# A fused four-layer kernel: FP4 decoding and an output projection moved between the attention and MLP stages, and a changed division of SSM passes in one batch

## Chip, cores and metric

The kernel runs on one core of one Trainium2 chip. The metric is device microseconds for one execution of the whole program. Five engines work side by side: TensorE (PE; PEld is its weight load), VectorE (DVE), ScalarE (ACT), GpSimd (POOL) and SyncE (SP, which here only issues transfers).

## What is computed

`x` is 4 batches of 512 rows by 512 columns in fp32. Four layers are added to it one after another:

```
x = x + ssm(ctx, layernorm(x))            # state-space scan, 512 channels, 16 states
x = x + experts(layernorm(x))             # top-1 of 32 masked ternary matrices
x = x + attention(layernorm(x), ctx)      # 32 heads of 16, softmax, @ Wout + bout
x = x + mlp(layernorm(x))                 # FP4 weights
# mlp: gate_up = x @ w_gu.T   (512 -> 2 x 1408);  h = silu(gate) * up
#      y = h @ w_down.T;  y / sqrt(mean(y*y) + 1e-6)
# FP4: eight 4-bit codes in an int32 word; value = code's number * fp16 scale of its group of 128
```

## The kernel before

The program is a row of stages: SSM, experts, attention, MLP. A stage is one or more blocks. In a block each engine has an instruction stream of its own and waits on semaphores; at a block's end the engines meet at a barrier, before which SP clears the block's semaphores one by one. `X` stays in SBUF as 16 tiles of 128 rows, 4 to a batch.

**SSM.** 128 passes g: 4 batches (32 passes each, g = 96 to 127 are the last batch) by 2 halves of the channels by 16 states. A pass has two 128x512 tiles, w = 0 and 1. ACT makes `dA` for both (L327); POOL makes `dBu` for both in one 128x1024 product (`weigh_states`, L363); DVE runs two scans (L464), and multiplies tile 0 by C into `hC` (L419); tile 1 is multiplied by POOL (`project`, L370), except in a *whole* pass, one in eight, where DVE does that one too. PE sums `hC` over the states (L258). POOL's order is `weigh_states(g + 2)`, `project(g)`. Near the middle of a batch DVE adds the second half's step sizes (`add_delta`, L393; for the last batch directly after pass 104) and weighs `u` (`weigh_u`, L399).

**Attention.** A prologue block loads weights and context (SP's queue), prepares a table, and adds the experts' first batch to `X`. Then one block per batch of `X` (names `att_first`, `att_next`). In a batch, projections come first, then a software pipeline over g = -2 to 8 with four steps kt each. At g, PE makes the scores of head group g + 2, whose maxima DVE takes (L1493), and the exponentials of group g are taken by ACT (L1390). For g = 6 and 7 no scores are left to make, so DVE has only the normalisation of heads (`normalise(g - 1)`, L1440 and L1443, at kt = 1) and, in the first batch, row statistics (L1458). The output projection of batch b - 1 is spread over the first steps of batch b's pipeline. The last batch's has a block of its own, `project_last`: four times a transpose of `heads` (L1525), a copy by ACT (L1539), a product with `Wout` (L1532), and an addition by DVE (L1546).

**MLP.** One block. SP first issues 32 transfers of the gate and up words (every word row goes to 8 partitions, 176 KB each), then 8 transfers of the down words (352 KB each) and one of the down scales (1408 KB). DVE takes the layer norm of batch 0, then decodes the four chunks g of gate and up words, each 128x2816, with three instructions (`codes`, L1750 to L1752). ACT turns each decoded chunk into fp16 (`Vgu`, L1713). PE's first unit needs chunk g for its group g. Then 22 units a batch: 8 products a unit (L1657, L1658), ACT evacuates groups 0 and 2 (L1725), DVE adds groups 1 and 3 (L1833), POOL adds the halves (L1631). During batch 0 DVE also decodes the down weights, one of 11 parts after every second unit; the first of these waits for all nine down transfers (`down_in`).

## Time and profile before

| | |
|---|---|
| median of 3 runs | 1810.77 us (1808.63 to 1811.18) |
| the profiled execution's own time | 1811.14 us |
| its span in the trace | 1809.3 us |
| PE busy | 1491.6 us, 82% |
| DVE busy | 1366.2 us, 76% |
| ACT busy | 911.2 us, 50% |
| POOL busy | 689.3 us, 38% |

The span runs from the first to the last instruction in the trace; the execution's own time is 1.84 us longer. Busy shares are means over stages with different limits, so they say which engine is used most, and not what bounds a given stage. All times in the rows below are microseconds from the span's start.

### The profile page before, as it was taken

Reading aid. Unit: us, or ns where it says so; the run is one execution under the profiler, and the core shown is the slowest. Engines: PE = TensorE matmul, PEld = TensorE weight load, DVE = VectorE, ACT = ScalarE, POOL = GpSimd, SP = SyncE. Lnnn points to the kernel's source line nnn. Section 1 sums busy time; section 2 is a strip of 40 time slices with the busy share of each in tenths; the row PEclk is TensorE's granted clock in tenths of the full one; section 3 lists DMA queues with packets and bytes.
Section 4 is the critical chain, followed back from the end, with each engine's and each line's share of the span. In section 5 each row is a group of like instructions: output and inputs, shape, how many; then the busy total and the mean of one; then the engine's idle time right before and its main releaser. Section 6 shows DMA issues by size and latency. Waiting matters only on the chain. (4 is left out here: it accounts for less than half of the span.)

```text
span 1809.3 us, 20906 instructions
## 1 busy us (share of the span) xinstructions
PE 1491.6 (82%) x6523; PEld 615.7 (34%) x6523; DVE 1366.2 (76%) x2030; ACT 911.2 (50%) x1201; POOL 689.3 (38%) x477
## 2 busy tenths in 40 slices
PE   5998998886654872899889988999899289898997
PEld 1333333332232321433343344324433134343433
DVE  6989999899988853789668756957792788647453
ACT  4766565664430100447655752776375353546453
POOL 3999999999925335000100010001001033333342
PEclk8898999988986996879999999999999699999999
DMA  6455455555568744300000000000000810000000
GB/s 237 127 149 146 142 144 144 149 149 137 147 187 180 157 96 157 123 1 1 1 1 1 1 1 1 1 1 1 1 1 1 178 46 1 24 1 24 1 24 24
DMA packets 65211, 131.54 MB, mean 73 GB/s; under 512 B 11328, under 2 KB 11328, under 8 KB 64336
## 3 DMA queue, kind: packets, MB, share of 16 engines
q1 hardware_dynamic: 53056, 104.07, 20.3%
q0 software_dynamic: 7168, 25.17, 6.1%
q10 hardware_dynamic: 4880, 0.95, 0.3%
q8 instruction: 57, 0.93, 0.2%
q14 instruction: 50, 0.41, 0.1%
HBM read 134.11 MB, written 12.85 MB: 81 GB/s over the span
## 5 line engine op out<-in xcount | busy, mean ns | idle before, releaser
L363 POOL TENSOR_TENSOR ssm_dBu<-ssm_du,ssm_BC 128x1024 f32<-128x1024 f32 x128 | 303.4, 2375 | 17.2 <-DVE ssm_du L399 17.2
L258 PE MATMUL ssm_psY<-ssm_hC,ident 128*128 128x512 f32 x512 | 256.0, 631 | 47.7 <-POOL ssm_hC L370 33.6
L1493 DVE TENSOR_REDUCE att_next_mx<-att_next_ring 128x1 f32<-128x512 f32 x384 | 242.0, 684 | 32.6 <-PE att_next_ring L1236 31.0
L327 ACT ACTIVATE ssm_dA<-ssm_delta,ssm_negA 128x512 f32<-128x512 f32 x256 | 165.4, 682 | 170.0 <-DVE ssm_hC L419 168.6
L1390 ACT ACTIVATE att_next_Pr<-att_next_psT 128x1024 f32<-128x1024 f32 x192 | 186.3, 1023 | 88.5 <-PE att_next_psT L1260 87.9
L1631 POOL TENSOR_TENSOR mlp_both<-mlp_first,mlp_third 128x512 f32<-128x512 f32 x88 | 124.3, 1412 | 256.9 <-DVE mlp_first L1833 166.1
L1833 DVE SCALAR_TENSOR_TENSOR mlp_first<-mlp_psQ,mlp_s_gu,mlp_first 128x512 f32<-128x512 f32 x176 | 131.4, 749 | 110.2 <-ACT mlp_first L1725 94.0
L1507 POOL TENSOR_TENSOR X<-X,att_bout 128x512 f32<-128x512 f32 x12 | 15.9, 1354 | 496.2 <-SPq L1141 496.2
L464 DVE TENSOR_TENSOR_SCAN ssm_dA<-ssm_dA,ssm_dBu 128x512 f32<-128x512 f32 x144 | 174.3, 1220 | 21.8 <-ACT ssm_dA L327 15.3
L1657 PE MATMUL mlp_psQ<-mlp_xh,mlp_Vgu 128*128 128x512 f16 x352 | 141.5, 402 | 50.4 <-ACT mlp_Vgu L1713 27.6
L258 PEld LDWEIGHTS ssm_psY<-ssm_hC,ident 128*128 128x128 f32 x512 | 96.5, 198 | 197.2 <-issue 93.6
L1668 PE MATMUL mlp_psD<-mlp_Wd,mlp_hT 128*128 128x512 f32 x352 | 157.4, 592 | 0.0
L370 POOL TENSOR_TENSOR ssm_hC<-ssm_dBu,ssm_BC 128x512 f32<-128x512 f32 x112 | 147.3, 1316 | 18.2 <-DVE ssm_dBu L464 17.4
L1658 PE MATMUL mlp_psQ<-mlp_xl,mlp_Vgu 128*128 128x512 f16 x352 | 140.9, 400 | 0.0
L464 DVE TENSOR_TENSOR_SCAN ssm_dBu<-ssm_dA,ssm_dBu 128x512 f32<-128x512 f32 x112 | 133.9, 1195 | 0.0
L1236 PE MATMUL att_next_ring<-att_KT,att_QT 64*128 64x512 f16 x384 | 119.1, 380 | 13.6 <-DVE att_next_mx L1493 9.3
L890 PE MATMUL moe_psO<-moe_W,moe_XST 128*128 (+1 forms) x376 | 98.4, 388 | 23.9 <-issue 17.9
L1725 ACT ACTIVATE mlp_first<-mlp_psQ,mlp_s_gu 128x512 f32<-128x512 f32 x88 | 60.2, 684 | 103.0 <-PE mlp_psQ L1658 100.3
L1270 PE MATMUL att_next_psO<-att_next_Pr,att_V 128*32 128x512 f32 x768 | 102.3, 604 | 1.1 <-ACT att_next_Pr L1390 1.1
L193 PE MATMUL ssm_psI<-ssm_ctxP,ssm_w_tap 128*128 128x512 f32 x192 | 97.2, 620 | 6.9 <-ACT ssm_delta L290 6.9
L419 DVE TENSOR_TENSOR ssm_hC<-ssm_dA,ssm_BC 128x512 f32<-128x512 f32 x144 | 94.6, 666 | 0.0
L1257 PE MATMUL att_next_psT<-att_QT,att_KT 64*128 64x512 f16 x384 | 92.3, 379 | 0.2
(316 smaller groups left out, 2488.2 us busy)
## 6 DMA issues: line engine op xcount, KB each, us to landing
ssm_BC<-bc_rows SPq DMA_DIRECT2D x128, 512.0 KB, 4.8
moe_W<-in_masksT POOLq DMA_DIRECT2D x32, 512.0 KB, 8.4
mlp_words<-in_gate_upT SPq DMA_DIRECT2D x32, 176.0 KB, 7.3
X<-in_x SPq DMA_DIRECT2D x4, 1024.0 KB, 10.7
rows<-moe_XP SPq DMA_DIRECT2D x4, 1024.0 KB, 14.6
out_x<-X SPq DMA_DIRECT2D x4, 1024.0 KB, 4.2
mlp_Wd<-in_downT SPq DMA_DIRECT2D x8, 352.0 KB, 14.8
ssm_ctxP<-in_ctxT SPq DMA_DIRECT2D x4, 512.0 KB, 12.3
```

Of the source, the lines that this page charges most:

```text
L258: nc.tensor.matmul(psY[:, w, :], ident[:], hC[:, w, g % RC, :], start=False, stop=(n == DS - 1)).then_inc(summed, 1)
L327: nc.scalar.activation(dA[:, q % RA, :], delta[:, b % 2, e, :], ACT.Exp, scale=negA[:, e, n:n + 1]).then_inc(dA_done, 1)
L363: nc.gpsimd.tensor_tensor(dBu[:, g % RB], du[:, b % 2, hh * W:(hh + 1) * W, :], BC[:, g % RING, 0, :].unsqueeze(1).broadcast_to([P, W, S]) ...
L370: nc.gpsimd.tensor_tensor(hC[:, 1, g % RC, :], dBu[:, g % RB, 1, :], BC[:, g % RING, 1, :], ALU.mult).then_inc(hC_done[1], 1)
L464: nc.vector.tensor_tensor_scan(h, dA[:, q % RA, :], dBu[:, g % RB, w, :], 0.0, ALU.mult, ALU.add).then_inc(h_done, 1)
L1390: nc.scalar.activation(Pr[:, i % NP_], psT[:, i % 2], ACT.Exp).then_inc(exp_done, 1)
L1493: nc.vector.tensor_reduce(mx[:, m % 3, qt, row_order(j)], bank(("score", i)), AX.X, ALU.max).then_inc(maxed, 1)
L1631: nc.gpsimd.tensor_tensor(both[:, w, :], first[:, w, :], third[:, w, :], ALU.add).then_inc(summed, 1)
L1657: nc.tensor.matmul(psQ[:, g, :], Vgu[:, g, cols], xh[:, g, :], start=True, stop=False)
L1658: nc.tensor.matmul(psQ[:, g, :], Vgu[:, g, cols], xl[:, g, :], start=False, stop=True).then_inc(grp, 1)
L1668: mm = nc.tensor.matmul(psD[:, t, :], hT[:, J % HT, t * P:(t + 1) * P], Wd[:, j, :], start=(j == 0), stop=(j == JT - 1))
L1833: nc.vector.scalar_tensor_tensor(out=first[:, w, :], in0=psQ[:, g, :], scalar=s_gu[:, row, g:g + 1], in1=first[:, w, :], op0=ALU.mult, op1 ...
```

## The change

- SSM: in the last batch (g from 96 on) a pass in four is whole, not one in eight. That makes passes 99, 107, 115 and 123 whole in addition to 103, 111, 119 and 127. `wholes(n)` counts them for the waits.
- The gate and up words come in one chunk per attention batch: the 8 transfers of chunk b are issued in batch b, into one buffer that chunks share. DVE decodes a chunk in two pieces of 1408 columns, at g = 6 and g = 7 (kt = 2). ACT turns chunk b - 1 into `Vgu` in batch b, at g = -1; chunk 3 in the MLP block. The shift constants are made in the attention prologue.
- `project_last` and its block are gone; the MLP block does that work: PE turns all four `heads` tiles, projects tiles 0 and 1, turns the normalised rows of batch 0, and projects tiles 2 and 3. `psD` is used as its PSUM.
- To make room, attention's `ctxT` holds two batches (batch b + 1's context is loaded in batch b), `Pr` is shared by all batches, and `xn` and the landing places of the experts' results lie in `Pr`, `Vgu` and `words`. So the fourth result is fetched with the others, with no wait, and the prologue's SP queue has two context transfers fewer.

```diff
-    FULL = 8
+    FULL, FULL_LAST = 8, 4
+    LAST = TOTAL - PER
...
-            return g % FULL == FULL - 1
+            every = FULL if g < LAST else FULL_LAST
+            return g % every == every - 1
+        def wholes(n):
+            return min(n, LAST) // FULL + max(n - LAST, 0) // FULL_LAST
...
-        ctxT = sb("ctxT", [P, B, CK, S])
+        ctxT = sb("ctxT", [P, 2, CK, S])
...
-        returned_to = (back, heads, xo, back)
...
+        Pr = sb("Pr", [P, NP_, 2, S])
+        Vgu, words, sign, shift, heads, xo, Wout, bout = (late.Vgu, late.words, late.sign, late.shift, late.heads, late.xo, late.Wout, late.bout)
+        xn = Pr[:, 0:2].rearrange("p i w s -> p (i w) s")
+        room = Vgu[:].rearrange("p g o -> p (g o)").bitcast(F32)
+        returned_to = (Pr[:, 2:4].rearrange("p i w s -> p (i w) s"), room[:, 0:NT * D].rearrange("p (t d) -> p t d", d=D),
+                       room[:, NT * D:2 * NT * D].rearrange("p (t d) -> p t d", d=D),
+                       words[:, 0:NT * D].bitcast(F32).rearrange("p (t d) -> p t d", d=D))
...
-                    for k in range(1, B - 1):
+                    for k in range(1, B):
                         fetch_back(k)
                     sp.dma_start(Wout[:], ins["Wout"].rearrange("(c p) n -> p c n", p=P)).then_inc(wout_in, 16)
                     sp.dma_start(bout[:], ins["bout"].partition_broadcast(P)).then_inc(wout_in, 16)
-                    for k in range(1, B):
-                        sp.dma_start(ctxT[:, k], ins["ctxT"][k].rearrange("(c p) s -> p c s", p=P)).then_inc(ctx_in[k], 16)
-                    sp.wait_ge(added, NT)
-                    fetch_back(B - 1)
+                    sp.dma_start(ctxT[:, 1], ins["ctxT"][1].rearrange("(c p) s -> p c s", p=P)).then_inc(ctx_in[1], 16)
...
+                        if 1 <= b < B - 1:
+                            sp.dma_start(ctxT[:, (b + 1) % 2], ins["ctxT"][b + 1].rearrange("(c p) s -> p c s", p=P)).then_inc(ctx_in[b + 1], 16)
                         if first:
-                            for k in range(1, B):
-                                sp.wait_ge(ctx_in[k], 16)
+                            sp.wait_ge(readded, TILES - NT)
+                        else:
+                            sp.wait_ge(late.gu_done, b)
+                        for k in range(PER):
+                            sp.dma_start(words[k:P:PER, :], ins["gate_upT"][b * P // PER:(b + 1) * P // PER, :]).then_inc(late.chunk_in[b], 16)
+                        if b + 1 < B:
+                            sp.wait_ge(ctx_in[b + 1], 16)
...
+                                if g == -1 and kt == 1 and b >= 1:
+                                    keep_codes(nc, act, late, b - 1)
...
+                        def decode(n):
+                            w, t2 = words[:, n * PIECE:(n + 1) * PIECE], sign[:]
+                            dve.wait_ge(late.chunk_in[b], 16 * PER)
+                            if 2 * b + n >= 1:
+                                dve.wait_ge(late.vals, 2 * b + n)
+                            chain.link(nc.vector.tensor_scalar(w, w, shift[:, 1:2], shift[:, 2:3], ALU.logical_shift_left, ALU.logical_shift_right))
+                            chain.link(nc.vector.tensor_scalar(t2, w, 1 << 12, 3, ALU.bitwise_and, ALU.logical_shift_left))
+                            nc.vector.scalar_tensor_tensor(out=w, in0=w, scalar=7 << 9, in1=t2, op0=ALU.bitwise_and, op1=ALU.bitwise_or).then_inc(late.vals, 1)
...
+                                if kt == 2 and NG - LAG <= g < NG:
+                                    decode(g - NG + LAG)
...
-        project_last(B - 1)
...
+def keep_codes(nc, act, late, g):
+    act.wait_ge(late.vals, 2 * (g + 1))
+    half = late.words[:].bitcast(F16).rearrange("p (o w) -> p o w", w=2)[:, :, 0]
+    nc.scalar.activation(late.Vgu[:, g, :], half, ACT.Copy, scale=2.0 ** 14).then_inc(late.gu_done, 1)
...
-                for g in range(DT):
-                    for k in range(PER):
-                        sp.dma_start(words[k:P:PER, g, :], ins["gate_upT"][g * 16:(g + 1) * 16, :]).then_inc(chunk_in[g], 16)
...
-                nc.gpsimd.iota(shift[:, 0:1], [[0, 1]], base=0, channel_multiplier=4).then_inc(consts, 1)
+                for t in range(NT):
+                    nc.gpsimd.tensor_tensor(X4[:, B - 1, t, :], X4[:, B - 1, t, :], bout[:], ALU.add).then_inc(biased, 1)
...
+                def turn_heads(t):
+                    for c in range(DT):
+                        mm = nc.tensor.transpose(psD[:, t, c * P:(c + 1) * P], heads[:, t, c * P:(c + 1) * P], ident[:])
+                    mm.then_inc(h_turned, 1)
+                def project_out(t):
+                    pe.wait_ge(xo_done, t + 1)
+                    for c in range(DT):
+                        mm = nc.tensor.matmul(psD[:, t, :], xo[:, c, t * P:(t + 1) * P], Wout[:, c, :], start=(c == 0), stop=(c == DT - 1))
+                    mm.then_inc(o_proj, 1)
...
+                for t in range(NT):
+                    turn_heads(t)
+                project_out(0)
+                project_out(1)
                 turn(0)
+                project_out(2)
+                project_out(3)
...
+                for t in range(NT):
+                    act.wait_ge(h_turned, t + 1)
+                    nc.scalar.activation(xo[:, :, t * P:(t + 1) * P], psD[:, t, :].rearrange("p (c k) -> p c k", c=DT), ACT.Copy).then_inc(xo_done, 1)
                 root_variances(0)
+                keep_codes(nc, act, late, DT - 1)
                 high_parts(0)
-                for g in range(DT):
-                    act.wait_ge(vals, g + 1)
-                    half = words[:, g, :].bitcast(F16).rearrange("p (o w) -> p o w", w=2)[:, :, 0]
-                    nc.scalar.activation(Vgu[:, g, :], half, ACT.Copy, scale=2.0 ** 14).then_inc(gu_done, 1)
-                act.wait_ge(consts, 2)
...
+                def add_projection(t):
+                    dve.wait_ge(biased, t + 1)
+                    dve.wait_ge(o_proj, t + 1)
+                    nc.vector.tensor_tensor(X4[:, B - 1, t, :], X4[:, B - 1, t, :], psD[:, t, :], ALU.add).then_inc(o_added, 1)
                 row_stats(0)
                 normalise(0)
-                low_parts(0)
-                for g in range(DT):
-                    dve.wait_ge(chunk_in[g], 16 * PER)
-                    codes(words[:, g, :], words[:, g, :], sign[:]).then_inc(vals, 1)
                 dve.wait_ge(scales_in, 16)
                 nc.vector.tensor_copy(s_gu[:], s_gu16[:]).then_inc(consts, 1)
-                dve.wait_ge(consts, 2)
+                add_projection(0)
+                add_projection(1)
+                low_parts(0)
+                add_projection(2)
+                add_projection(3)
+                dve.wait_ge(consts, 1)
                 for b in range(B):
                     for u in range(UNITS):
```

## Rows read from the trace of the kernel before

**Rows 1.** Chain of waits, pieces from the MLP: start us, duration us, what.
```profile
1408.22 0.63 SPq L1613
...
1441.57 3.10 DVE mlp_words L1752
...
1566.92 3.43 PE mlp_psD L1668 x8
1573.88 3.43 PE mlp_psD L1668 x8
...
1619.13 1.75 PE mlp_psQ L1642 x16
```

**Rows 2.** Windows: stretch, length, each engine's busy us (count), PEclk, DMA share, GB/s.
```profile
1408.22:1448.10 39.88, 7.45 (x24) 3.91 (x25) 34.42 (x36) 14.94 (x12) 0.13 (x1) 0.56 1.01 205
...
1427.00:1454.00 27.00, 8.72 (x24) 2.38 (x24) 20.52 (x13) 13.12 (x12) 2.53 (x2) 0.56 1.04 237
```

**Rows 3.** Timeline of all engines around the last output projection: start us, us, instruction, idle before.
```profile
1379.11 0.26 DVE L1440 RECIPROCAL att_next_rec<-att_next_ring 128x16 f32<-128x16 f32 x1 [8.26 <-PE att_next_ring L1278]
...
1386.09 0.26 DVE L1440 RECIPROCAL att_next_rec<-att_next_ring 128x16 f32<-128x16 f32 x1 [6.26 <-PE att_next_ring L1278]
...
1389.16 4.94 POOL L1551 TENSOR_TENSOR X<-X,att_bout 128x512 f32<-128x512 f32 x4 [161.80 <-SPq L1517]
1389.18 1.94 PE L1525 MATMUL att_last_psH<-ident,att_heads 128*128 128x128 f32 x8 [3.13 <-PEq L64]
...
1411.82 0.17 DVE L1761 TENSOR_SCALAR mlp_mv<-mlp_mv 128x4 f32<-128x4 f32 x1
```

**Rows 4.** Groups of instructions by form: busy us, mean ns; idle before.
```profile
L1752 DVE SCALAR_TENSOR_TENSOR mlp_words<-mlp_words,mlp_sign 128x2816 int32<-128x2816 int32 x4 | 12.4, 3093 | 0.1
...
L1713 ACT ACTIVATE mlp_Vgu<-mlp_words 128x2816 f16<-128x2816 f16 x4 | 10.2, 2550 | 19.8 <-DVE mlp_words L1752 19.8
...
L1752 DVE SCALAR_TENSOR_TENSOR mlp_td<-mlp_td 128x512 int32<-128x512 int32 x11 | 7.6, 693 | 0.4
...
L1750 DVE TENSOR_SCALAR mlp_words<-mlp_words,mlp_shift 128x2816 int32<-128x2816 int32 x4 | 7.0, 1746 | 0.5 <-DMA mlp_words<-in_gate_upT 0.4
...
L1751 DVE TENSOR_SCALAR mlp_sign<-mlp_words 128x2816 int32<-128x2816 int32 x4 | 6.5, 1627 | 0.1
```

**Rows 5.** Timelines of the MLP's first units.
```profile
1450.82 0.69 ACT L1725 ACTIVATE mlp_third<-mlp_psQ,mlp_s_gu 128x512 f32<-128x512 f32 x1 [0.91 <-PE mlp_psQ L1658]
...
1456.24 1.49 DVE L1750 TENSOR_SCALAR mlp_td<-mlp_Wd,mlp_shift 128x512 int32<-128x512 int32 x1
```

**Rows 6.** Timeline of ScalarE in the last attention batch.
```profile
1296.06 1.94 ACT L1390 ACTIVATE att_next_Pr<-att_next_psT 128x1024 f32<-128x1024 f32 x2 [12.49 <-PE att_next_psT L1260]
```

**Rows 7.** Timeline of VectorE at the end of the first attention batch.
```profile
883.65 0.26 DVE L1440 RECIPROCAL att_first_rec<-att_first_ring 128x16 f32<-128x16 f32 x1 [1.54 <-PE att_first_ring L1278]
```

**Rows 8.** Timeline of all engines in the attention prologue.
```profile
716.90 2.74 DVE L1038 SCALAR_TENSOR_TENSOR X<-att_back,gate,X 128x512 f32<-128x512 f32 x4 [1.80 <-DMA att_back<-results]
...
722.87 3.19 SPq L997 DMA_DIRECT2D att_ctxT<-in_ctxT  x3
...
726.11 1.31 SPq L985 DMA_DIRECT2D att_back<-results  x1
728.55 1.00 DVE L1408 TENSOR_SCALAR att_first_xn<-X,att_mv,att_rstd 128x512 f32<-128x512 f32 x2 [5.33 <-PEq L64]
```

**Rows 9.** Timelines of VectorE and GpSimd in the SSM stage.
```profile
37.33 1.23 DVE L393 TENSOR_TENSOR ssm_delta<-ssm_delta,ssm_acc 128x1024 f32<-128x1024 f32 x1 [0.60 <-ACT ssm_acc L297]
...
421.91 5.81 DVE L393 TENSOR_TENSOR ssm_delta<-ssm_delta,ssm_acc 128x1024 f32<-128x1024 f32 x1
...
446.44 2.34 DVE L464 TENSOR_TENSOR_SCAN ssm_dA<-ssm_dA,ssm_dBu 128x512 f32<-128x512 f32 x2
...
492.42 1.23 DVE L464 TENSOR_TENSOR_SCAN ssm_dA<-ssm_dA,ssm_dBu 128x512 f32<-128x512 f32 x1 [0.61 <-POOL ssm_dBu L363]
...
430.04 1.26 POOL L370 TENSOR_TENSOR ssm_hC<-ssm_dBu,ssm_BC 128x512 f32<-128x512 f32 x1 [3.41 <-DVE ssm_dBu L464]
```

More of the change, by code:

```diff
@@ L2 @@
 from contextlib import ExitStack
+from dataclasses import dataclass
 import concourse.bass as bass
@@ L925, in stage_experts, with stage_attention @@
         sp_.clear()
-def stage_attention(nc, X, ident, ident16, gate, results, ins):
+def stage_attention(nc, X, ident, ident16, gate, results, late, ins):
     H, HD = 32, 16
@@ L943, in stage_attention @@
     PI = math.pi
+    NP_ = 4
+    GU = late.Vgu.shape[-1]
+    PIECE = GU // 2
+    PER = 8
     with ExitStack() as ctx:
@@ L978, in stage_attention @@
             turns_f = c_.sb("turns_f", [P, 2, TILES, FQ])
-            pos_in, added, consts, own, mv_done, rooted, ang_done, sin_done = (c_.sem(n) for n in (
-                "pos_in", "added", "consts", "own", "mv_done", "rooted", "ang_done", "sin_done"))
+            pos_in, added, numbered, consts, own, mv_done, rooted, ang_done, sin_done = (c_.sem(n) for n in (
+                "pos_in", "added", "numbered", "consts", "own", "mv_done", "rooted", "ang_done", "sin_done"))
             with nc.Block() as block:
@@ L1057, in stage_attention @@
         LAG = 2
-        NP_ = 4
         WIDE = D // 2
@@ L1180, in project @@
                                 for c in range(CK):
-                                    mm = nc.tensor.matmul(out, ctxT[:, b, c, rows], Wkv[:, c, 0:D], start=(c == 0), stop=(c == CK - 1))
+                                    mm = nc.tensor.matmul(out, ctxT[:, b % 2, c, rows], Wkv[:, c, 0:D], start=(c == 0), stop=(c == CK - 1))
                             else:
@@ L1556, in stage_attention, with late_tiles, stage_mlp @@
             batch(b, b - 1, f"next{b}")
-        project_last(B - 1)
-def stage_mlp(nc, X, ident, stored, ins, out):
+@dataclass
+class Late:
+    Vgu: object
+    words: object
+    sign: object
+    shift: object
+    heads: object
+    xo: object
+    Wout: object
+    bout: object
+    vals: object
+    gu_done: object
+    chunk_in: object
+def late_tiles(nc, ctx):
+    GU = 2 * 11 * P
+    sb = Space(nc, ctx, "late").sb
+    return Late(sb("Vgu", [P, DT, GU], F16), sb("words", [P, GU], I32), sb("sign", [P, GU // 2], I32), sb("shift", [P, 3], I32),
+                sb("heads", [P, NT, D]), sb("xo", [P, DT, S]), sb("Wout", [P, DT, D]), sb("bout", [P, D]),
+                ctx.enter_context(nc.semaphore("late_vals")), ctx.enter_context(nc.semaphore("late_gu_done")),
+                [ctx.enter_context(nc.semaphore(f"late_chunk_in{i}")) for i in range(DT)])
+def keep_codes(nc, act, late, g):
+    act.wait_ge(late.vals, 2 * (g + 1))
+    half = late.words[:].bitcast(F16).rearrange("p (o w) -> p o w", w=2)[:, :, 0]
+    nc.scalar.activation(late.Vgu[:, g, :], half, ACT.Copy, scale=2.0 ** 14).then_inc(late.gu_done, 1)
+def stage_mlp(nc, X, ident, stored, late, ins, out):
     JT = 11
@@ L1570, in stage_mlp @@
         sb, sem = m_.sb, m_.sem
-        Vgu = sb("Vgu", [P, DT, GU], F16)
         Wd = sb("Wd", [P, JT, D])
@@ L1594, in stage_mlp @@
         psD = m_.ps("psD", [P, NT, D])
+        Vgu, shift, heads, xo, Wout, bout, gu_done = (late.Vgu, late.shift, late.heads, late.xo, late.Wout, late.bout, late.gu_done)
         X4 = X[:].rearrange("p (b t) d -> p b t d", t=NT)
@@ L1598, in stage_mlp @@
         out4 = out.rearrange("b (t p) d -> p b t d", p=P)
-        consts, own, vals, gu_done = sem("consts"), sem("own"), sem("vals"), sem("gu_done")
-        chunk_in = [sem(f"chunk_in{i}") for i in range(DT)]
+        consts, own = sem("consts"), sem("own")
+        h_turned, xo_done, o_proj, biased, o_added = (sem(n) for n in ("h_turned", "xo_done", "o_proj", "biased", "o_added"))
         down_in, scales_in, mv_done, rooted, rstd_done = (sem(n) for n in ("down_in", "scales_in", "mv_done", "rooted", "rstd_done"))
@@ L1913, in program @@
         stage_experts(nc, X, ident, ident16, gate, (rows, results), (rows_fetched, rows_returned, masks_in), ins)
-        stage_attention(nc, X, ident, ident16, gate, results, ins)
-        stage_mlp(nc, X, ident, stored, ins, out)
+        late = late_tiles(nc, ctx)
+        stage_attention(nc, X, ident, ident16, gate, results, late, ins)
+        stage_mlp(nc, X, ident, stored, late, ins, out)
 def kernel(**inputs):
```

94 lines of the change are left out of this document (27 added, 67 removed).

## The prediction, made before the changed kernel was run

> **What bounds the kernel now.** I read the chain of waits first, since it names what set the end. Its MLP part [rows 1] starts with SP issuing the word transfers at 1408.22, goes through DVE's last decoding instruction at 1441.57, and turns into PE work only after that; in the later batches it is the down products, 6.97 us from one group to the next. The windows say how empty PE is until then: 7.45 us busy in the 39.88 us from 1408.22 to 1448.10 [rows 2]. The timeline just before shows the last output projection with PE nearly alone, and, in the batch that ends there, DVE idle for 8.26 and 6.26 us before the last two normalisations [rows 3]. So three serial pieces stand in a row (projection, layer norm, decoding), while the engine that decodes has free time some microseconds earlier.
>
> **The MLP's start, worked out.** The new block begins where the old projection block did, at 1389.2. On PE it runs:
> - 16 transposes of `heads`. Eight took 1.94 with the clock low, after 3.13 us of idle [rows 3]; I take 3.7 for 16.
> - Four projections of eight products each. Eight products of this shape (128x512, fp32) take 3.43 at the high clock, as the MLP's down products show [rows 1]. Four are 13.7.
> - 16 transposes of the normalised rows: 1.75 at the high clock [rows 1].
>
> Together 19.2 us, so unit 0 starts at 1408.4. The other engines must be done by then. ACT: four copies of 0.6, ending at 1393.7; then a root, to about 1395.3; then one chunk, 2.55 [rows 4], to about 1397.9. DVE: the statistics, which in the old block were through 3.8 us after its start at 1408.2 [rows 3], so at 1393.0; the normalisation after the root, some 2 us, until 1397.4, before PE asks for it at 1399.8. POOL's additions end at 1394.1 [rows 3], before that normalisation. All are hidden behind PE; without that cover the ACT series would be worth 8.7 us, and it would have to grow by over 2 us to delay PE's turn.
>
> Now the same point in both kernels. Before, ACT's evacuation of unit 1's third group started at 1450.82 [rows 5]. A unit is (6.97 - 3.43) / 2 = 1.77 us of PE [rows 1]. Following groups from 1408.4: unit 0 ends at 1410.2, unit 1's second and third groups wait for evacuations of about 0.7 each on ACT and DVE, and the same evacuation starts at about 1411.6. The difference is 39.2 us. That takes in the removed block with its boundary, the 32 issues, the four decodings and the four ACT copies but one.
>
> The next thing that could be late is the down weights. Before, DVE took them at 1456.24 [rows 5], which becomes 1417.0. SP issues them from 1389.2 on; they are 8 x 352 KB and 1408 KB, 4.3 million bytes, which at 237 GB/s [rows 2] need 18.2 us, so they are there at about 1409. Hidden, with 8 us to spare.
>
> **The decodings in the attention batches.** VectorE's third instruction takes 3093 ns for 2816 columns and 693 for 512 [rows 4], so 1.04 ns a column and 0.16 us fixed, and 1.62 us for 1408. Half of the other two, 0.87 and 0.81, with 0.1 each for the fixed part: a piece is 3.6 us with its waits. The bounds are 3.2 (exact half) and 6.5 (no saving). In batches 1 to 3, 3.6 goes into the idle times of 8.26 and 6.26 [rows 3]: nothing; at 6.5 the second piece would cost 0.2 a batch. In the first batch, row statistics already fill part of these, and only 1.54 us are idle before the last normalisation [rows 7]. So the block ends 3.6 - 1.5 = 2.1 later (0 to 5). The transfers land long before: the chunk's eight issues are 0.63 each [rows 1]. The ACT copy of 2.55 stands in a stretch of 12.49 us without work for ACT [rows 6]: nothing.
>
> What would make the decoding slow is GpSimd. In the SSM stage an addition of two SBUF operands takes 1.23 us with GpSimd idle and 5.81 with it busy [rows 9]. At the ends of attention batches GpSimd does nothing (it sat idle 161.80 us until 1389.16 [rows 3]), so I take the undisturbed price. The Trainium skill ("SBUF — State Buffer", section "Who interferes with whom") says that VectorE in a two-port mode, or with two SBUF inputs, and GpSimd lock each other out for whole instructions. The trace agrees on the addition. If GpSimd worked where the pieces go, 4.6 us more on each of eight would turn the gain of 42 below into some 5; it does not work there, so the rule leaves the sum as it is, and its case goes with the second rival.
>
> **The attention prologue.** DVE's last work there is over at 723.2, but the next block starts at 728.55 after 5.33 us idle [rows 8]: the end of SP's queue (726.11 + 1.31 = 727.42) sets it. The change removes two of the three context issues, 3.19 / 3 = 1.06 each, and moves the fourth result up. An issue of 1.31 for one transfer, where the first ones of a queue take 0.6, is one held back by transfers in flight, and of these there is 1 MB less. So I take 2.5 off, a little over the two issues' 2.1; the bounds are 2.1 and 4.2 (DVE's end, 727.42 - 723.2). The four new DVE instructions of about 0.2 and the index instruction lie ahead of the wait for results, where DVE idles 1.80 [rows 8]: nothing; up to 0.8 without it. Five more semaphores are cleared at block ends, an estimate of 0.06 each: +0.3.
>
> **The SSM part.** Passes 99, 107, 115 and 123 take a product from POOL (1.26, spacing 1.23) and give DVE one (two scans take 2.34 and the two products 1.27, so one product is +0.6) [rows 9]. Neither engine bounds the batch alone. Up to pass 104 DVE works almost without a gap. Then its `add_delta` runs from 421.91 to 427.72, freed when POOL runs out of work at 426.63 and waits 3.41 until 430.04 [rows 9]. With pass 99 whole POOL gets there 1.0 earlier (1.23, less because pass 104's scan comes 0.6 later): -1.0. From there DVE has three more products, +1.8, and idle gaps such as 0.61 before 492.42 [rows 9], five of these and some small ones, 3.3 together, that POOL's 3.7 us less work closes: -1.5. Sum -2.5. Bounds: -4.9 if POOL alone set the pace (4 x 1.23), +2.4 if DVE did and nothing is recovered.
>
> **Sum.** -39.2 - 2.5 - 2.5 + 2.1 + 0.3 = -41.8. Against the profiled execution's own 1811.14 that is 1769.3; the median of the runs is 0.37 lower, so about 1769.
>
> **Rivals.**
> - *The small stages give nothing back* (SSM +2.4, prologue 0, first batch +4): the MLP gain with +6.7, so -32.5, 1778. For it: DVE is without gaps for most of the last SSM batch. Against it: the gaps of 0.61 in its last eight passes [rows 9], where POOL is late. 0.13 for something in 1773 to 1779.
> - *The decoding costs its whole price in attention*, since some wait I have not seen puts DVE or ACT on the path: 8 x 3.6 and 3 x 2.55 are 36.5 us, of which 2.1 are counted; 1769 + 34 = 1803. Pieces slowed by 4.6 each would come to about the same. Against it: the idle times [rows 3, 6]. 0.04.
> - *The MLP's start is limited by something other than PE*: the down weights (a stall begins if they need over 27.8 us, so below 156 GB/s against the row's 237), or ACT's series in front of the transposes. Some 3 to 12 us, 1772 to 1781. 0.10.
> - *More is gained*: SSM at POOL's pace and a prologue ending with DVE, 4 us more, 1761 to 1765. 0.08.
> - *Slower than before.* The chunk's transfer lies behind a wait of its own on SP for ACT's copy in batches 1 to 3. If it landed after g = 6, DVE would stand in front of its last two normalisations, and the batch with it. To lose 42 us the three batches must stand 14 us each: landing later than about 1385 in the last batch, 100 us after ACT's copy, while 1.4 MB at 205 GB/s [rows 2] need 7. 0.01 for slower by over 0.2%, 0.01 for no change. 0.2% of the time is 3.6 us, about what a measurement can tell.
>
> The forecast itself gets 0.63, with 1765 to 1773 as its own range. For 8 in 10 I take in the lower part of the first and third rival and the fourth: 1763 to 1778.
>
> **What the profile should show.** No output projection block, and the MLP's first DVE instruction at about 1386.6 (1389.2 - 2.5 - 2.5 + 2.1 + 0.3). Unit 0 on PE 19 us after it, with PE over 85% busy in between and the high clock from about 4 us on. The down decoding without a wait for its transfers. Eight pieces of about 3.6 us on DVE in idle times, with the normalisations of batches 1 to 3 at unchanged distances; the first batch about 2 us longer. The first attention block 2.5 us sooner after the prologue's start. The SSM stage 2.5 us shorter, with DVE without gaps to its end. The forecast is wrong if unit 0 waits for `Vgu` or for the normalised rows, if the down weights come after unit 1, or if a decoded piece takes much over 4 us.

## The result, and the profile after

The changed kernel took 1765.33 us (median of four runs, 1764.84 to 1765.78) and the kernel before 1810.97, a ratio of 0.975 with a 95% interval of 0.9733 to 0.9767. The profiled execution took 1765.17 us with a span of 1763.0, against 1811.14 and 1809.3 before. The prediction was 1769 us with a range of 1763 to 1778, so the total is inside; two of its terms, the SSM stage and the prologue, lie outside their own bounds, as the stages show.

The spans differ by 46.3 us. I cut both executions at the same instructions (the first of VectorE in a stage or batch, the last additions to X of the SSM stage, the first down decoding of the MLP) and took the differences, minus meaning sooner:

| stretch | predicted | measured |
|---|---|---|
| SSM stage | -2.5 | -6.2 |
| experts' stage | 0 | +0.4 |
| attention prologue | -2.5 | -1.1 |
| first attention batch | +2.1 | +1.9 |
| the three batches after it | +0.3 (semaphores) | +1.1, +0.4, +0.3 |
| first MLP instruction to the first down decoding (before: from the projection block's start) | -39.2 | -39.0 |
| from there to the end | 0 | -4.1 |

The chain of waits of the changed kernel, where the MLP starts (start us, duration us, what), answers to [rows 1]:

```profile
1385.89 3.47 PE mlp_psD L1656 x16
1389.36 7.00 PE mlp_psD L1662 x16
1396.37 1.75 PE mlp_psQ L1672 x16
1398.11 6.87 PE mlp_psD L1662 x16
1404.98 0.22 PE mlp_psQ L1687
...
1414.09 1.42 DVE mlp_td L1788
```

PE now works without a break from the block's start to unit 0 at 1404.98, 19.1 us later; the prediction had 19.2. The windows say it again (columns as in [rows 2]): PE is busy for 19.11 of 19.11 us, where in [rows 2], which begins with the old MLP block and not with the projection, it was 7.45 of 39.88. The second row is the MLP from its first down decoding to the end, the third the experts' stage up to its first product with the cumulated rows:

```profile
1385.89:1405.00 19.11, 19.11 (x65) 11.20 (x66) 10.44 (x22) 8.39 (x11) 4.95 (x4) 0.91 1.00 199
1414.01:1763.00 348.99, 314.52 (x1073) 131.36 (x1071) 223.62 (x336) 173.45 (x276) 121.92 (x86) 0.97 0.03 13
505.31:538.25 32.94, 17.27 (x129) 12.29 (x129) 31.50 (x77) 15.39 (x28) 6.24 (x21) 0.81 0.97 265
```

The timeline shows what the projection hides (start us, us, engine, instruction, idle time before it): statistics, root, the copy of the last chunk's codes, and the issue of the down weights all lie beside PE's first 11 us.

```profile
1385.89 2.47 DVE L1796 BATCH_NORM_STATS2 mlp_stats<-X 128x6 f32<-128x512 f32 x4 [2.52 <-PEq L65]
...
1386.17 5.69 SPq L1633 DMA_DIRECT2D mlp_Wd<-in_downT  x8
...
1391.42 2.53 ACT L1581 ACTIVATE late_Vgu<-late_words 128x2816 f16<-128x2816 f16 x1
...
1391.76 1.92 DVE L1810 TENSOR_SCALAR mlp_xb<-X,mlp_mv,mlp_rstd 128x512 f32<-128x512 f32 x4
...
1405.09 0.69 DVE L1846 TENSOR_TENSOR X<-X,mlp_psD 128x512 f32<-128x512 f32 x1 [2.75 <-PE mlp_psD L1662]
```

The decoding pieces by form, answering to [rows 4]; the columns are busy us, mean ns and idle time before. A piece is 1.00 + 0.89 + 1.63, with the gaps 3.59 us from its first start to its last end (3.6 predicted).

```profile
L1501 DVE SCALAR_TENSOR_TENSOR late_words<-late_words,late_sign 128x1408 int32<-128x1408 int32 x8 | 13.0, 1626 | 0.3
...
L1581 ACT ACTIVATE late_Vgu<-late_words 128x2816 f16<-128x2816 f16 x4 | 10.2, 2547 | 0.0
...
L1499 DVE TENSOR_SCALAR late_words<-late_words,late_shift 128x1408 int32<-128x1408 int32 x8 | 8.0, 1004 | 0.0
...
L1500 DVE TENSOR_SCALAR late_sign<-late_words 128x1408 int32<-128x1408 int32 x8 | 7.2, 894 | 0.3
```

At the end of the first batch the last normalisation now starts with no idle time before it, where [rows 7] had 1.54:

```profile
872.64 1.63 DVE L1501 SCALAR_TENSOR_TENSOR late_words<-late_words,late_sign 128x1408 int32<-128x1408 int32 x1
...
878.89 0.25 DVE L1464 RECIPROCAL att_first_rec<-att_first_ring 128x16 f32<-128x16 f32 x1
```

The prologue's end, answering to [rows 8]. SP's last issue is over at 720.48, VectorE's last instruction at 717.79, so SP still sets when the batch starts:

```profile
709.49 5.15 SPq L997 DMA_DIRECT2D late_words<-results  x1
714.68 2.57 SPq L1006 DMA_DIRECT2D late_Wout<-in_Wout  x1
717.30 2.58 SPq L1007 DMA_DIRECT2D late_bout<-in_bout  x1
719.92 0.56 SPq L1008 DMA_DIRECT2D att_ctxT<-in_ctxT  x1
```

```profile
717.61 0.18 DVE L1061 RECIPROCAL att_rstd<-att_rstd 128x4 f32<-128x4 f32 x1
721.67 1.00 DVE L1432 TENSOR_SCALAR att_Pr<-X,att_mv,att_rstd 128x512 f32<-128x512 f32 x2 [3.88 <-PEq L65]
```

In the SSM stage `add_delta` of the last batch, 5.81 us in [rows 9], takes 2.30: it is issued 0.06 us after GpSimd began a product, and runs after it, before GpSimd's next instruction, which takes 3.33 instead of 2.35 us.

```profile
422.09 2.30 DVE L400 TENSOR_TENSOR ssm_delta<-ssm_delta,ssm_acc 128x1024 f32<-128x1024 f32 x1
```

```profile
422.03 1.28 POOL L377 TENSOR_TENSOR ssm_hC<-ssm_dBu,ssm_BC 128x512 f32<-128x512 f32 x1
423.26 3.33 POOL L370 TENSOR_TENSOR ssm_dBu<-ssm_du,ssm_BC 128x1024 f32<-128x1024 f32 x1
```

### The profile page after: what moved, and what is told of

It is laid out like the page before. It is cut to its first block and busy times, and to the rows that moved or that the text cites. A ratio compares the mean times of both kernels' runs of the same rounds, so it can differ in the third digit from the quotient of the medians.

```text
span 1763.0 us, 20903 instructions
## 1 busy us (share of the span) xinstructions
PE 1483.3 (84%) x6523; PEld 612.0 (35%) x6523; DVE 1366.0 (77%) x2046; ACT 910.9 (52%) x1201; POOL 687.1 (39%) x473
## 5 line engine op out<-in xcount | busy, mean ns | idle before, releaser
L1527 DVE TENSOR_REDUCE att_next_mx<-att_next_ring 128x1 f32<-128x512 f32 x384 | 241.8, 683 | 32.7 <-PE att_next_ring L1258 31.0
L1412 ACT ACTIVATE att_Pr<-att_next_psT 128x1024 f32<-128x1024 f32 x192 | 186.2, 1023 | 81.2 <-PE att_next_psT L1282 80.5
L1543 POOL TENSOR_TENSOR X<-X,late_bout 128x512 f32<-128x512 f32 x12 | 15.9, 1354 | 498.4 <-POOLq L65 498.4
L471 DVE TENSOR_TENSOR_SCAN ssm_dA<-ssm_dA,ssm_dBu 128x512 f32<-128x512 f32 x148 | 178.3, 1217 | 18.2 <-ACT ssm_dA L334 14.2
L1687 PE MATMUL mlp_psQ<-mlp_xh,late_Vgu 128*128 128x512 f16 x352 | 137.7, 391 | 22.6 <-DVE mlp_first L1873 16.7
L377 POOL TENSOR_TENSOR ssm_hC<-ssm_dBu,ssm_BC 128x512 f32<-128x512 f32 x108 | 142.8, 1323 | 15.8 <-DVE ssm_dBu L471 14.8
L1688 PE MATMUL mlp_psQ<-mlp_xl,late_Vgu 128*128 128x512 f16 x352 | 136.7, 388 | 0.0
L471 DVE TENSOR_TENSOR_SCAN ssm_dBu<-ssm_dA,ssm_dBu 128x512 f32<-128x512 f32 x108 | 128.8, 1192 | 0.0
L1292 PE MATMUL att_next_psO<-att_Pr,att_V 128*32 128x512 f32 x768 | 102.3, 604 | 1.1 <-ACT att_Pr L1412 1.1
```

What stands on the lines that cost most here:

```text
L377: nc.gpsimd.tensor_tensor(hC[:, 1, g % RC, :], dBu[:, g % RB, 1, :], BC[:, g % RING, 1, :], ALU.mult).then_inc(hC_done[1], 1)
L471: nc.vector.tensor_tensor_scan(h, dA[:, q % RA, :], dBu[:, g % RB, w, :], 0.0, ALU.mult, ALU.add).then_inc(h_done, 1)
L1412: nc.scalar.activation(Pr[:, i % NP_], psT[:, i % 2], ACT.Exp).then_inc(exp_done, 1)
L1527: nc.vector.tensor_reduce(mx[:, m % 3, qt, row_order(j)], bank(("score", i)), AX.X, ALU.max).then_inc(maxed, 1)
L1687: nc.tensor.matmul(psQ[:, g, :], Vgu[:, g, cols], xh[:, g, :], start=True, stop=False)
L1688: nc.tensor.matmul(psQ[:, g, :], Vgu[:, g, cols], xl[:, g, :], start=False, stop=True).then_inc(grp, 1)
```

## The experiments

All start from the changed kernel; the name in brackets is that of the run. Times of a stretch are from the profiled execution of each.

**The SSM edit undone (e1).** The four whole passes of the last batch become those of before.

```diff
-    FULL, FULL_LAST = 8, 4
+    FULL, FULL_LAST = 8, 8
```

> The changed kernel with the SSM edit alone undone (one whole pass in eight also in the last batch). Theory A, the comparison of the two traces: the whole difference of the SSM stage hangs on these four passes, so its last addition to X comes at 508.0 us as before (501.86 in the changed kernel), add_delta of the last batch takes 5.8 us again and not 2.3, and the total is 6.2 us up, 1771.5, within 3 us for what the moved phase does to TensorE's clock in the MLP. Rival, the prediction's own price: 2.5 us, 1767.8. If the stage ends at 508.0 and the total is up by over 9, the clock part of theory A has to be looked at.

Measured: 1771.15 us (four runs, 1768.28 to 1773.10). From the last batch's first `add_delta` to the last additions to X the stage takes 130.55 us (before 130.51, changed kernel 124.14), and the second `add_delta` takes 5.81 again. So the SSM term is 6.4 us by this measure, and all of it is these passes. Its total, 5.8 above the first group of runs and 3.1 above the changed kernel's second group (below), is consistent with that but says little: the groups of one kernel differ by 3 us.

**Pass 99 alone (e2).**

```diff
-            every = FULL if g < LAST else FULL_LAST
-            return g % every == every - 1
+            return g % FULL == FULL - 1 or g == LAST + 3
```

> The changed kernel, but in the SSM's last batch only pass 99 is whole beside those of before (103, 111, 119, 127): passes 107, 115 and 123 are split again. Theory A (one event: because GpSimd is one product ahead, VectorE's add_delta gets in after GpSimd's current instruction and doesn't wait until GpSimd runs dry): add_delta takes about 2.3 us, and the stage's last addition comes at 508.0 - 3.3 = 504.7. Rival (each whole pass gives the same): a quarter of 6.2, so 506.5, and add_delta takes about 4.8.

The same stretch takes 127.00 us, and the addition takes 2.27:

```profile
421.27 2.27 DVE L399 TENSOR_TENSOR ssm_delta<-ssm_delta,ssm_acc 128x1024 f32<-128x1024 f32 x1
```

One whole pass gives 3.5 of the 6.4 us, through one instruction; passes 107, 115 and 123 give the other 2.9 together; no run separates them. Theory A holds for its part. The prediction had -1.0 and -1.5 at these two places. The one run took 1769.36 us.

**The second `add_delta` one pass later (e3).**

```diff
+                    if j == 9:
+                        add_delta(b, 1)
                     project(g, 0)
...
-                    if j == 8:
-                        add_delta(b, 1)
-                    if j == 9:
+                    if j == 10:
                         weigh_u(b, 1)
```

> The changed kernel with the second add_delta of each batch issued one pass later, after the two scans of pass j = 9, where in batches 1 and 2 GpSimd is in its short product (191.2 to 192.5 in batch 1, VectorE there at about 192.3), and not at the end of pass j = 8, where GpSimd is in the second of two long ones; weigh_u follows one pass later too. Theory A (what GpSimd is doing when the addition is issued decides): the addition takes 1.3 to 2.5 us in batches 1 and 2 and not 5.8, and each of these batches ends about 3.3 us sooner, 6.6 in all, 1758.7. In batch 0 and in the last one GpSimd's phase is another; not forecast, 0 to 3.5 each. Rival (an addition of two SBUF operands always waits until GpSimd has run out of work unless GpSimd is already short of it): 5 to 6 us again, no change, 1765.3.

My rule for when the addition gets in fell. Rows of VectorE from batches 0 and 1 and, under them, GpSimd's around them; then the same for batch 2:

```profile
78.78 2.29 DVE L400 TENSOR_TENSOR ssm_delta<-ssm_delta,ssm_acc 128x1024 f32<-128x1024 f32 x1
```

```profile
192.15 6.88 DVE L400 TENSOR_TENSOR ssm_delta<-ssm_delta,ssm_acc 128x1024 f32<-128x1024 f32 x1
```

```profile
77.65 2.34 POOL L370 TENSOR_TENSOR ssm_dBu<-ssm_du,ssm_BC 128x1024 f32<-128x1024 f32 x1
79.96 2.26 POOL L377 TENSOR_TENSOR ssm_hC<-ssm_dBu,ssm_BC 128x512 f32<-128x512 f32 x1
```

```profile
192.08 2.34 POOL L370 TENSOR_TENSOR ssm_dBu<-ssm_du,ssm_BC 128x1024 f32<-128x1024 f32 x1
194.38 1.26 POOL L377 TENSOR_TENSOR ssm_hC<-ssm_dBu,ssm_BC 128x512 f32<-128x512 f32 x1
195.61 2.34 POOL L370 TENSOR_TENSOR ssm_dBu<-ssm_du,ssm_BC 128x1024 f32<-128x1024 f32 x1
201.96 1.26 POOL L377 TENSOR_TENSOR ssm_hC<-ssm_dBu,ssm_BC 128x512 f32<-128x512 f32 x1 [4.01 <-DVE ssm_dBu L471]
```

```profile
308.55 7.10 DVE L400 TENSOR_TENSOR ssm_delta<-ssm_delta,ssm_acc 128x1024 f32<-128x1024 f32 x1
```

```profile
307.45 1.28 POOL L377 TENSOR_TENSOR ssm_hC<-ssm_dBu,ssm_BC 128x512 f32<-128x512 f32 x1
```

In batch 0 the addition was issued 1.1 us into one of GpSimd's long products and ran after it (2.29 us, 7.60 in the kernels so far). In batch 1 it was issued 0.07 us into one and was passed over for two further instructions, until GpSimd had nothing to do (6.88 us). In batch 2 it was issued where theory A wanted it, in a short product of GpSimd (1.1 us in), and took 7.10 us all the same; the last batch was like the first (2.36). Neither the kind of GpSimd's instruction nor the time since its start separates these from the cases above. And the 5.3 us less in batch 0 hardly shortened the way to the next batch: from one first `add_delta` to the next it took 106.6 us, where the other profiles, with 7.6 us for the addition, have 105.5 to 107.0. The median was 1769.79 (four runs, 1766.95 to 1772.13).

**Three transfers later (e5), and passes 35 and 67 whole too (e8).** First the transfers alone (`Wout`, `bout` and the context of batch 1 are issued at the start of the first attention batch):

```diff
-                    sp.dma_start(Wout[:], ...)
-                    sp.dma_start(bout[:], ...)
-                    sp.dma_start(ctxT[:, 1], ...)
...
                         if first:
+                            sp.dma_start(Wout[:], ...)
+                            sp.dma_start(bout[:], ...)
+                            sp.dma_start(ctxT[:, 1], ...)
                             sp.wait_ge(readded, TILES - NT)
```

> The changed kernel with three transfers (Wout, bout, the context of batch 1) issued by SP at the start of the first attention batch and not at the end of the prologue. Theory A (the prologue ends when SP has issued its last transfer, and each issue is held back by those in flight): SP is through at 714.6 and not at 720.5, so VectorE's end at 717.8 decides, and the first batch starts 2.7 us sooner, at 719.0 after 721.67; total 1762.6. Rival 1: the block ends later for another reason (its boundary, ACT), and nothing is gained. Rival 2: the transfers now compete with or precede something in the first batch and what is gained is given back there: 1765.3.

From the prologue's first VectorE instruction to the first normalised rows 14.01 us, against 17.33 in the changed kernel: 3.3 us less. The batch's first instruction now comes 1.06 us after VectorE's last in the prologue, where it was 3.88:

```profile
722.16 1.00 DVE L1432 TENSOR_SCALAR att_Pr<-X,att_mv,att_rstd 128x512 f32<-128x512 f32 x2 [1.06 <-PEq L65]
```

The first batch took 161.1 us, as in the changed kernel, so nothing is given back. Theory A holds. The median, 1764.59 (1762.61 to 1767.42), hides it in the spread that c1 below explains. Then the passes:

```diff
+    WHOLE = {g for g in range(TOTAL) if g % FULL == FULL - 1 or g >= LAST and g % FULL_LAST == FULL_LAST - 1} | {PER + 3, 2 * PER + 3}
```

> e5 (three transfers issued in the first attention batch) with passes 35 and 67 of the SSM stage whole too, the fourth pass of batches 1 and 2, as pass 99 is of the last batch. Theory A (the one product less puts GpSimd's phase where VectorE's addition gets in, worth 3.5 us by the run with pass 99 alone): the second add_delta of batches 1 and 2 takes 2.3 us and not 5.8, each of the two batches takes 112.6 us from one first add_delta to the next and not 116.0, and the total is 3.3 + 6.8 below the changed kernel's, some 1755. Rival (in batches 1 and 2 something other than VectorE or GpSimd is late after it, as in batch 0, where in the run with the later addition 5.3 us less on it gave back only 0.4): under 1 us a batch, 1761 to 1762.

Both additions take 2.3 us now, as theory A had it, but the two batches became shorter by 0.7 and 0.3 us only. The waits of VectorE from the second addition of batch 1 to the first of batch 2 say where it went: with the passes, and in the changed kernel's second profile (engine, line waited for, us in total, times, longest):

```profile
DVE ssm_yo L436 <- PE ssm_psY L265: 4.2, 1, 4.2
```

```profile
DVE ssm_yo L436 <- PE ssm_psY L265: 1.4, 1, 1.4
```

VectorE now waits 4.2 us for PE's sums instead of 1.4. PE is busy for 66 of the 70 us of that stretch, since it also makes the next batch's projections; in the last batch, which has no next one, for 55 of 78 in the changed kernel. There the addition was on the path, here PE is. The rival holds. Median 1762.49 (five runs, 1761.25 to 1763.96), ratio 0.9725 (0.9712 to 0.9738).

**The changed kernel again (c1).**

> The changed kernel itself, for a second profile of it and for more times. Theory A: parts of the time differ from execution to execution of one kernel, because TensorE's clock is lowered at other moments: in the profiles so far the MLP from its first down decoding to the end took 348.9 to 349.0 us in three kernels and 352.1 to 352.2 in two, with the same code there, and the experts' stage 197 to 199 or 203 us. So the 4.07 us that the MLP's rest gained belongs to no part of the change; this profile shows 349 or 352 there, and 199 or 203, whatever the first one showed, and the times spread over more than 3 us. Rival: each kernel has its own value: 349.0 and 199.0 again within 0.3 us, and times within 1 us of each other.

Five runs: 1765.34 to 1771.45, median 1768.05, ratio to before 0.9752 (0.9735 to 0.9769). The windows of this second profile, the same two stretches as in the windows above:

```profile
1416.54:1768.72 352.18, 316.31 (x1073) 132.00 (x1071) 223.50 (x336) 173.68 (x276) 121.73 (x86) 0.96 0.03 12
```

```profile
504.73:542.78 38.05, 22.59 (x128) 15.72 (x129) 31.68 (x77) 15.54 (x28) 9.40 (x27) 0.63 0.91 241
```

352.18 us where the first profile had 348.99, and 38.05 where it had 32.94, with a PEclk of 0.63 instead of 0.81. Nothing in the code differs. PE's products after a like idle time show it; first the first profile, then the second (products that start 0.2 us apart are at the high clock, those 0.4 apart at the low one):

```profile
1452.42 0.39 PE L1687 MATMUL mlp_psQ<-mlp_xh,late_Vgu 128*128 128x512 f16 x1 [2.06 <-DVE mlp_first L1873]
...
1454.38 0.38 PE L1688 MATMUL mlp_psQ<-mlp_xl,late_Vgu 128*128 128x512 f16 x1
1454.59 0.38 PE L1687 MATMUL mlp_psQ<-mlp_xh,late_Vgu 128*128 128x512 f16 x1
```

```profile
1455.38 0.39 PE L1687 MATMUL mlp_psQ<-mlp_xh,late_Vgu 128*128 128x512 f16 x1 [2.01 <-DVE mlp_first L1873]
...
1457.23 0.63 PE L1688 MATMUL mlp_psQ<-mlp_xl,late_Vgu 128*128 128x512 f16 x1
1457.65 0.63 PE L1687 MATMUL mlp_psQ<-mlp_xh,late_Vgu 128*128 128x512 f16 x1
```

Idle for 2.06 us in the one and 2.01 in the other, and the clock falls from 2.4 to 1.2 GHz for some 3 us in the second alone. Over all profiles the MLP's last stretch took 348.8 to 349.3 us in eight and 352.1 to 353.1 in four, the kernel before among these; the experts' stretch 32.7 to 33.2 in three with nothing added, 35.3 in one and 37.9 to 38.1 in six. Theory A holds for 3.2 of the 4.1 us at the end, which come and go between two profiles of one kernel. For the other 0.9, between the slower profiles of the changed kernel (352.1 to 352.2) and the only one of the kernel before (353.1), there is only a hint: after the first down decoding and before 1590, windows show PEclk at 0.50 to 0.51 for 3.4 us from each of 1432.7, 1456.5 and 1514.6 in the second profile, in the kernel before for 3.4, 3.4 and 6.8 us from 1460.8, 1494.9 and 1552.9, and in the first profile for 6.8 us from 1416.8 alone.

**The merge undone (e6).** The old projection block stands before the MLP block again, and the MLP starts with the layer norm:

```diff
+        project_last(B - 1)
...
-                for t in range(NT):
-                    turn_heads(t)
-                project_out(0)
-                project_out(1)
                 turn(0)
-                project_out(2)
-                project_out(3)
```

> The changed kernel with the merge alone undone: the last output projection stands in a block of its own again, and the MLP block starts with the layer norm of batch 0; the gate and up codes are still decoded in the attention batches. It divides the 39.0 us. Theory A: the old block costs 19.0 us with its boundary, but the merged start only hides the layer norm under the projection, so undoing it costs the layer norm's chain (statistics 3.8, root 1.5, chunk copy 2.6, four copies 2.4, products after): from the first DVE instruction after the last batch to the first down decoding 38 us and not 28.1, so +10 (8.4 to 11), and the decoding's move is worth the other 29. Rival: the whole block was saved, +19, and the decoding's move is worth 20.

From the last batch's first instruction to the first down decoding: 208.15 us, against 195.15 in the changed kernel's second profile and 234.15 before. So the merge is worth 13.0 us and the decoding's move 26.0. The one run took 1781.52 us. Both expectations missed, and the rows say by what (PE's first unit, and the first down decoding):

```profile
1417.75 0.38 PE L1730 MATMUL mlp_psQ<-mlp_xh,late_Vgu 128*128 128x512 f16 x1 [1.46 <-ACT mlp_xh L1765]
```

```profile
1430.47 0.55 DVE L1820 TENSOR_SCALAR mlp_td<-mlp_Wd,late_shift 128x512 int32<-128x512 int32 x1 [3.79 <-DMA mlp_s_d<-in_down_scales]
```

Unit 0 starts at 1417.75, 28.2 us after the projection block's start at 1389.51 and not 19.1 after: 9.1 us, inside the 8.4 to 11 for the layer norm's chain. The other 3.8 are the wait of VectorE for the down weights, which SP can only issue when the MLP block starts at 1408.4; the last of them lands 22.0 us later.

**Decoding left out (e4).**

```diff
-                            chain.link(nc.vector.tensor_scalar(w, w, shift[:, 1:2], shift[:, 2:3], ...))
-                            chain.link(nc.vector.tensor_scalar(t2, w, 1 << 12, 3, ...))
-                            nc.vector.scalar_tensor_tensor(out=w, ...).then_inc(late.vals, 1)
+                            nc.vector.tensor_scalar(w, w, 7 << 9, 0, ALU.bitwise_and, ALU.bitwise_or).then_inc(late.vals, 1)
```

> The changed kernel with one short instruction (0.8 us) in place of the three of each decoded piece (3.5 us) in the attention batches; the gate and up weights are then wrong. Theory A, the prediction's: only the first batch pays for the decoding, so it takes 159.1 us and not 161.0, and the batches after it stay at 168, 167.3 and 167.3 within 0.4. The 1.1 us by which the second batch grew stay, since they come with 3.4 us more of the low clock. Rival: the decoding costs in every batch: the second 1.1 us shorter, at 167.4, the third and fourth 0.3 each, at 167.0.

The first batch took 159.47 us (161.02 with the decoding), the others 167.73, 167.08 and 167.18, against 167.71, 167.06 and 167.18 in the changed kernel's second profile. Only the first batch pays, 1.6 us for the 2.7 that each piece lost; its length in the profiles with the decoding is 160.5 to 161.5, so the 1.6 is good to about half a microsecond. Theory A holds for the first batch. Of the second batch's 1.1 us only 0.3 stay, here and in c1; the other 0.8 go with the granted clock at its start: a mean of 0.73 to 0.75 over the first 9.3 us in the first profile, e2 and e9 (168.5 us), and of 0.81 or 0.82 in the other eight, this one and c1 among them (167.7 to 167.8). The one run took 1763.31 us.

**PE kept busy (e9).** 28 transposes of the identity at the start of the experts' stage, which nothing reads:

```diff
+                for i in range(28):
+                    nc.tensor.transpose(psO[:, i % 2, 0:P], ident[:], ident[:])
                 pe.wait_ge(loaded, 32)
```

> The changed kernel with 28 transposes of the identity on PE at the start of the experts' stage, where PE stands idle for 11.3 us; nothing reads what they write, and at the high clock (0.22 us each) they take 6 of the 7 us until PE's first work there. Measured so far: from the stage's first VectorE instruction to PE's first product with the cumulated rows 32.7 to 33.2 us in three kernels, with 13.7 us of the low clock, and 37.9 to 38.1 in three others, with 24 us of it, the same code after the same 11.3 us of idle time. Theory A (after a stretch of idle time PE's clock is low for one of two lengths, and it is idleness that brings it): with the filling the low clock is gone or short, the stretch takes 29 to 33 us in the profile, and the times of the runs have a median 3 to 7 us below the changed kernel's 1768.1 and 1765.3. Rival 1 (the low clock comes back anyway): 33 or 38 again, no change. Rival 2 (the fillers run at the low clock, 12 us, and delay PE's first work by 5): slower by up to 5 us.

```profile
505.32 4.75 PE L907 MATMUL moe_psO<-ident 128*128 128x128 f32 x28 [4.19 <-PEq L65]
512.40 1.09 PE L855 MATMUL moe_psO<-ident,moe_XP 128*128 128x128 f32 x8 [2.33 <-DVE moe_XP L740]
```

```profile
505.31:538.24 32.93, 20.72 (x157) 15.50 (x157) 31.51 (x77) 15.12 (x28) 6.22 (x21) 0.91 0.98 265
```

PE's idle time before its first work falls from 11.3 to 2.3 us and PEclk rises to 0.91, but the stretch takes 32.93 us, as in the best cases without filling. The 28 transposes took 4.75 us; the 0.22 us each that the expectation gives for the high clock is the rate at the low one (16 in 3.47 us at 1385.89), and at the high clock 16 take 1.75. The chain there is VectorE's (31.5 of 33 us busy), and PE's clock is on it only when it is low for long. Five runs: 1763.35 to 1767.68, median 1764.31, which is 3.7 below the changed kernel's second group and 1.0 below its first. One profile can't show that the bad case is gone.

**All together (e10):** e8 with this filling and with 46 transposes in the attention prologue.

> The version that the runs point to: e8 (three transfers issued in the first attention batch, passes 35 and 67 whole), with the 28 transposes at the start of the experts' stage, and 46 more in the attention prologue, where PE stands idle for 34 us and the first batch then has 16 us of the low clock in its first 17. Theory A: 3 to 7 us less in the experts' stage, and the first batch, of which PE is a part of the chain only in its first 15 us, 2 to 4 us shorter than 161.0; with e8's 1762.5 that makes 1752 to 1757. Rival 1: the low clock comes back anyway, 1762.5. Rival 2: the first batch's start is VectorE's (rotations), so only the experts' stage gives something, 1756 to 1760.

Median 1758.71 us (five runs, 1757.63 to 1760.57), ratio to before 0.9713 (0.9694 to 0.9733), the fastest kernel of the study and in the range of rival 2. The experts' stretch took 32.92 us again, 5.2 less than in e8's profile. The first batch took 161.05 us, unchanged. My "16 us of the low clock in its first 17" was wrong: I had set the clock's record some 10 us too late against the instructions, in all the expectations that give a length of the low clock (the lengths stand, their places don't). The windows give a PEclk of 0.54 for the first 4.8 us of this batch in e8 and 1.00 after that, so there was little to win; here it is 0.61 over the first 5.1. The prologue took 15.99 us instead of 14.26: VectorE got the first of the experts' results 8.6 us after its first instruction there, and 6.9 us in e8. The transposes are what this block has more than e8's, but that they delay the result is not shown by one profile of each. They gave nothing that the profile shows; a version without them was not tried.

## Why the prediction was right, and where it was not

The total owes something to errors that cancel: the SSM term was 3.7 us too small and the prologue's 1.4 too large. And the first four runs lie 2.7 us below the next five of the same kernel, so the 3.7 us between forecast and first median say little about the terms; the stages do.

**The MLP's start** was right in its steps: PE is the bound, 19.1 us against 19.2, with ACT and VectorE hidden behind it. The down weights were issued from 1386.17 on. The last transfer, that of the scales, was issued at 1391.90 and landed 17.5 us later, so all were there at 1409.4, 23.2 us after the first issue, where I had worked out 18.2 from 237 GB/s (without the merge, in e6, it was 22.0). With 28 us until they are needed, 4.7 were to spare and not 8. The division between the parts is not simple: 9.1 us of layer norm hidden under the projection, 3.8 of down weights issued 19 us earlier, 26.0 of decoding.

**The decoding in attention** was right: price (3.59 against 3.6), place (only the first batch pays) and size (+1.9 against +2.1).

**The SSM term was mis-sized**, -6.2 against -2.5, and outside its bounds of -4.9 to +2.4. The step that failed is "with pass 99 whole POOL gets there 1.0 earlier: -1.0". It took `add_delta` to end when GpSimd runs out of work. With GpSimd's phase changed by one product, VectorE got in ahead of GpSimd's next instruction and never waited that long; pass 99 alone measured -3.5. The 1.0 itself does not follow from its bracket either: 1.23 less 0.6 is 0.6. My lower bound, four products of GpSimd, had no room for a lock that goes the other way. The Trainium skill ("SBUF — State Buffer", section "Who interferes with whom") says that whoever issues first gets the shared pair for the whole instruction. The rows agree that a waiting addition starts only when an instruction of GpSimd has ended, but not that coming first is enough: the one issued at 192.15 in e3 was passed over by two GpSimd instructions that started later, at 194.38 and 195.61. The rest, -2.9 against -1.5, has two parts. From the addition to the end of the stage VectorE's idle time fell from 5.9 to 2.0 us, by 3.9 where I had 3.3; and its busy time fell by 2.5, which is 3.5 for the addition less 1.0 for three more products, which I had put at 1.8. The windows of e2, which has the short addition without these products, give VectorE 75.44 us there against 78.96 before and 76.47 in the changed kernel.

**The prologue was mis-sized**, -1.1 against -2.5, and by less than its bound of 2.1. The failed step is that the back-pressure would weaken with one megabyte less in flight. SP had issues of 5.19, 2.62 and 3.19 (for three) behind the results; it now has 5.15, 2.57 and 2.58. The slow issues moved to the transfers that now stand in that place, and what was saved was a few short ones. That SP's end is what the batch waits for was right: with three issues moved away the prologue became 3.3 us shorter.

**The experts' stage and the MLP's rest** had no term. They differ by 5.1 and by 3.2 us between two executions of one kernel, in which only TensorE's granted clock is seen to differ; in the first profile of the changed kernel both were short. The terms that can be put down to the change, with 0.5 for the three later batches as in the second profile, add up to -39.0 - 6.2 - 1.1 + 1.9 + 0.5 = -43.9. The five later runs gave 1811.76 - 1768.05 = 43.7; predicted were 41.8.

**Open:** which of VectorE's two-operand additions get in between two GpSimd instructions and which wait for GpSimd to run dry. The runs show cases of both, and I found no rule that holds for all.

## What to carry to other kernels

Look for serial pieces that stand before a stage because they wait for a block boundary, and for time in which their engine idles earlier; a batch that is bound by another engine takes them in at no cost, up to the length of each idle interval. Before an instruction's shortening is counted, ask what its engine would wait for next: the same 3.5 us on the same instruction were worth 3.5 in the last SSM batch and 0.3 to 0.7 in those in which PE was the next bound. And a gain of some microseconds in one profile needs a second profile of the same kernel, cut at the same instructions.

## What the runs showed of the hardware that I had not expected

- After the same idle time of PE (11.1 to 11.3 us) the same code in the experts' stage ran with a mean granted clock of 0.76 to 0.81 (33 us), 0.69 (35 us, once) or 0.63 (38 us); after 2.0 to 2.1 us in the MLP the clock fell in some executions and not in others.
- A VectorE addition of two SBUF operands that takes 1.23 us alone took 2.3, 5.8, 6.9, 7.1 or 7.6 beside a row of GpSimd instructions, and one GpSimd instruction less, some 15 us earlier, changed 5.8 to 2.3.
- The eighth transfer that SP issues in the prologue took 5.0 to 5.6 us to issue, and the next two 2.6 each where they followed at once, whichever transfer stood there; in e5, issued some 4 us after that long issue had ended, the same two took 0.37 and 0.66.
